# Six instead of four of a batch's sixteen chunks weighted on ScalarE in a graph-attention stage

## What is computed

```python
x_proj = (x @ W).reshape(n, H, D)            # H = 8 heads, D = 32
alpha_src = jnp.einsum('nhd,hd->nh', x_proj, a_src)
alpha_dst = jnp.einsum('nhd,hd->nh', x_proj, a_dst)
e = alpha_src[row] + alpha_dst[col]
m = jax.ops.segment_max(e, col, num_segments=n)
e_exp = jnp.exp(e - m[col])
s = jax.ops.segment_sum(e_exp, col, num_segments=n)
att = e_exp / (s[col] + 1e-16)
out = jax.ops.segment_sum(att[:, :, None] * x_proj[row], col, num_segments=n)
```

## Time and profile before

| what | value |
|---|---|
| median of 3 runs | 3672.1 us (3669.44 to 3673.27) |
| profiled execution, its own time | 3671.94 us |
| its span | 3670.2 us |
| span, share busy: PE, DVE, ACT, POOL | 76%, 50%, 26%, 47% |
| granted PE clock, mean | 0.875 of full speed |

### The profile page before, as it was taken

One profiled execution on the slowest core, in us unless ns is written; L12 is line 12 of the kernel. 1 busy time (PEld: TensorE's weight loads), 2 busy tenths in 40 slices (PEclk: granted clock), 3 DMA queues, 4 the chain that ended last, 5 costly groups with the idle time before them and its releaser, 6 DMA issues. The chain is left out here.

```text
span 3670.2 us, 56109 instructions
## 1 busy us (share of the span) xinstructions
PE 2801.8 (76%) x13194; PEld 2306.5 (63%) x13195; DVE 1850.6 (50%) x4258; ACT 965.1 (26%) x3415; POOL 1719.0 (47%) x1811
## 2 busy tenths in 40 slices
PE   1477888887874999999995647766776776738999
PEld 0356666666663888888884535555555555538998
DVE  5324454444556111111113758778887778773444
ACT  0001110000010222222221334333443333325554
POOL 0677777777770222232221177766666667200000
PEclk9888888888887999999997868888888888857999
DMA  5333333333330222222222543333333333100000
GB/s 170 94 105 110 110 116 110 110 109 110 109 108 15 81 81 86 83 86 83 85 84 84 171 110 106 104 103 101 100 102 103 102 102 104 43 17 9 20 21 20
DMA packets 152206, 327.38 MB, mean 89 GB/s; under 512 B 38743, under 2 KB 89905, under 8 KB 147938
## 3 DMA queue, kind: packets, MB, share of 16 engines
q0 software_dynamic: 85824, 236.38, 22.8%
q1 hardware_dynamic: 59762, 83.04, 6.8%
q10 hardware_dynamic: 6480, 6.42, 0.5%
HBM read 286.42 MB, written 41.40 MB: 89 GB/s over the span
## 5 line engine op out<-in xcount | busy, mean ns | idle before, releaser
L633 POOL DMA_INDIRECT G<-g_rows,srcT x784 | 743.1, 948 | 426.3 <-issue 237.2
L633 POOL DMA_INDIRECT G<-h_rows,srcT x784 | 752.3, 960 | 251.8 <-issue 237.0
L1728 PE MATMUL pS<-G,O 128*128 x2336 | 639.2, 437 | 56.9 <-DVE O L1876 55.8
L817 PE MATMUL pS<-G,O 128*128 x2336 | 569.7, 408 | 142.2 <-SPq L804 108.6
L817 PEld LDWEIGHTS pS<-G,O 128*128 128x128 f32 x2336 | 476.4, 206 | 231.9 <-issue 153.3
L1728 PEld LDWEIGHTS pS<-G,O 128*128 128x128 f32 x2336 | 492.6, 214 | 199.4 <-issue 83.3
L1361 PE MATMUL pH<-XT,w1s 128*128 128x256 f32 x1728 | 384.0, 381 | 0.9 <-DVE XT L1401 0.9
L1371 PE MATMUL pY<-w2s,HE 128*128 128x256 f32 x1728 | 381.9, 379 | 0.0
L1361 PEld LDWEIGHTS pH<-XT,w1s 128*128 128x128 f32 x1728 | 329.8, 191 | 46.5 <-issue 1.3
L1386 ACT ACTIVATE HE<-pH,b1s 128x256 f32<-128x256 f32 x432 | 204.9, 474 | 583.2 <-PE pH L1361 583.2
L1293 POOL DMA_INDIRECT y_rows<-YE,yidx x108 | 109.3, 1012 | 527.3 <-DVE YE L1413 510.8
(11 more groups left out here) (301 smaller groups left out, 3535.2 us busy)
## 6 DMA issues: line engine op xcount, KB each, us to landing
w1s<-in_W_dram SPq DMA_DIRECT2D x16, 1024.0 KB, 5.2
w2s<-in_W_dram SPq DMA_DIRECT2D x16, 1024.0 KB, 8.0
G<-h_rows,srcT POOLq DMA_INDIRECT x784, 2.7
Y<-y_rows SPq DMA_DIRECT2D x49, 256.0 KB, 4.4
G<-g_rows,srcT POOLq DMA_INDIRECT x784, 2.8
g_rows<-OUT SPq DMA_DIRECT2D x49, 132.0 KB, 2.5
h_rows<-ACC SPq DMA_DIRECT2D x7, 896.0 KB, 5.4
X<-in_x_dram SPq DMA_DIRECT2D x1, 6144.0 KB
```

The lines of the kernel that those rows point to most:

```text
L633: pool.indirect_dma_start(out=G[:, c % (ring * Q), 0:width], out_offset=None, in_=rows, in_offset=bass.IndirectOffsetOnAxis(ap=srcT[:, c:c ...
L817: mm = nc.tensor.matmul(pS[k][:, 0:W], O[:, k, q, :], G[:, bass.ds((s % R0) * Q + q, 1), :].rearrange("p a d -> p (a d)"), start=(q == 0), ...
L1728: mm = nc.tensor.matmul(pS[:, bass.ds((w % BANKS) * BANK, NR)], O[:, k, q, :], G[:, bass.ds((s % R) * Q + q, 1), 0:NR].rearrange("p a d -> ...
```

## The change

`SHARE`, the number of chunks of a batch that ACT weights, goes from 4 to 6. DVE's one instruction then covers 10 chunks instead of 12 (2560 elements per partition instead of 3072), and ACT issues 48 instructions per batch instead of 32. Nothing else is edited.

```diff
             RB = R // z.BS
-            SHARE = 4
+            SHARE = 6
             PAIR_STEPS = 12
```

## The result

The changed kernel takes 3640.82 us (median of 6, 3638.37 to 3646.55) against 3671.32 us for the kernel before on the same chip: a ratio of 0.9916, 95% interval 0.9906 to 0.9926, or 30.5 us less. The forecast was 3639 us, the range 3628 to 3657. The profiled execution has a span of 3639.0 us, 31.2 less than before.

A forecast was written before the change was run, and what follows sets the result against it. The prediction took the stage from batch 3 on to be one chain on DVE. DVE's shorter chain (25 us) plus PE's clock (8 us) made 33 us off 3672.1, giving 3639 us, range 3628 to 3657.

The forecast's parts named there:

- DVE's saving: L1950 on DVE loses 512 of 3072 elements at 1.038 ns each: 0.53 us per batch.
- slow pairs: PE's second pairs taking 9.32 us instead of 7.64, in 14 batches of two pairs; DVE then waits about 1.2 us.
- It counts from batch 2 on: L1950's saving is lost to gather waits in batches 0 and 1, counts in batches 2 to 48: 25 us.
- ACT's work costs nothing: ACT's block grows 3.44 us per batch to 10.32, inside its 5.25 us idle before `fac`; costed at nothing.
- The overhead: Between ACT's block and `fac`: waiting for its products, signalling PE and entering the loop, between 0 and 1.58 us.
- The cover of 1.30 us: DVE first reads `fac` in L1858, 1.30 us after it ended, so a `fac` 0.30 us late is covered.
- The Trainium skill's rule: Puts multiplications on VectorE, not ScalarE, so speaks against the change; if the moved work lay on the chain, 143 us more.
- The last batch: Without DVE's scans `fac` comes 2.4 to 4.0 us late, 3.6 of it covered: 0 to 0.4 us, taken as 0.
- PE's clock: Shorter idle before PE's second pairs leaves fewer at the low clock: 8 us gained, bounds 17 gained to 12 lost.
- The long batches: Batches of two pairs lasting 26.59 to 26.71 us instead of 25.39, in 14 cases.
- Gathers: Rival: POOL's gathers bind in the one-pair batches and take the gain back, 3668 us; chance 0.06.
- Slower by a late `fac`: Rival: ACT's longer block holds `fac` back, DVE held up 1.8 us per batch, 3733 us; chance 0.04.

The follow-up runs named there:

- e1: Changed kernel (six chunks on ACT) with two dummy products on DVE behind L1950, some 0.53 us per batch: 3670.94 us, ratio 0.9991 to the kernel before.
- e6: Changed kernel (six chunks on ACT) with four dummy 128x128 products on PE at the start of each pair: 3639.38 us, ratio 0.9913 to the kernel before.
- e5: Kernel before (four chunks on ACT) with four dummy 128x128 products on PE at the start of each pair: 3658.46 us, ratio 0.9967.
- e3: Changed kernel with SHARE set to seven chunks on ACT instead of six: 3628.07 us, ratio 0.9873 to the kernel before.
- e4: Changed kernel with SHARE set to eight chunks on ACT instead of six: 3699.49 us, ratio 1.0068 to the kernel before.
- e2: Changed kernel (six chunks on ACT) with four chunks in the last batch alone: 3640.14 us, ratio 0.9910 to the kernel before.
- e10: Kernel before (four chunks) with two dummy products on DVE behind L1950, some 0.53 us longer per batch: 3688.46 us, ratio 1.0044.
- e11: Kernel before (four chunks) with one dummy product on DVE behind L1950, some 0.27 us longer per batch: 3682.98 us, ratio 1.0031.

## Why the prediction was right, and where not

- *DVE's saving.* Worked out 0.53 us per batch, measured 3356 - 2823 = 533 ns. e1 shows that it is the cause; e6 against e5 shows it without slow pairs (22.2 us).
- *It counts from batch 2 on.* EX(2) came 0.75 us earlier only, and L1950 still waited 24.6 us in four places, nearly all in batches 0 to 2. Right but for batch 2 itself, where L1950's wait grew from 2.16 to 2.75 us and took its saving back.
- *ACT's work costs nothing.* Block 10.27 us (10.32 worked out), rest 1.33 (1.28). The overhead, bounded by 0 and 1.58 us, is 0.33. The cover of 1.30 us is shown by e3 (used, not exceeded) and e4 (exceeded, 1.70 us each). Right. The Trainium skill's rule, page "ScalarE: Activation LUTs", section "Rules for kernel authors", which puts multiplications on VectorE, did not decide. The rows bear out its order and no more: a chunk takes 1.72 us on ACT and 0.27 on DVE, but e3 carries seven chunks on ACT at a gain.
- *The last batch* was the step that failed: 0 to 0.4 us was costed, 2.69 came. The working had `fac` right (DVE waited 1.44 us for it), but it took the 2.26 us that DVE next waits for PE as room. It overlooked that PE's products of the last batch come directly behind that batch's weighting, so that `s_prep_act`, elsewhere a batch early, is the last to arrive. PE started 3.06 us later, and DVE's wait for it grew to 3.38. PE's 9.30 us wait names it, e2 removes it.
- *PE's clock*: +8 was taken, 8.5 to 9.1 remain by subtraction and 10.9 by e5 and e6, but the reason given was wrong. Not every idle before a second pair shrank: the longest fell from 2.82 to 2.37 us, that of batch 26 grew from 1.35 to 1.59, since PE's first pair keeps its start but not its length. The counts of 14, 2, 5 and 0 to 2 for four to seven chunks, and 11 and 2 with DVE made longer, follow no order in DVE's time. The long batches were also read too narrowly, from two of them: the 14 last 26.57 to 27.04 us, not 26.59 to 26.71. What is shown: the slow pairs exist, cost up to 14 us in the kernel before (e5), come with a granted clock of 0.82 in the second pair (1.00 in the pairs of 7.64 us), and change in number with the batches' length. What isn't: why the low clock lies where it does, and how to tell their number ahead. The value fell well by luck inside bounds that were rightly kept at -12 to +17.
- *Gathers* did not take the gain back: the score copies waited for them five times before and five times after (60.2 and 57.8 us in all), and POOL's wait still stands at 50.8 us. *Slower by a late `fac`*: DVE waited for `fac` in L1858, which the prediction had named as a sign of being wrong, but only in the last batch.

## What to carry to other kernels

When an engine's program is the chain, price what it sheds by its own slope and look at the receiving engine's first reader: idle behind the block, plus how long the result lies before it is read, is the room there is; with the 0.33 us that the run with six showed, it gave seven as the most here before seven and eight were run. Look at the last iteration by itself, because what is a whole iteration early in the loop can be last there; a different split for that iteration alone took 5.5 us off the tail with seven chunks. And a wait for an engine is room only if that engine isn't itself held back by the change. Where another engine's clock rises and falls within the loop, give its term both signs: taking 0.53 us off DVE's chain cut the slow pairs from 14 to 5, but taking 0.27 off e10's raised them from 2 to 11 (e11).

## What was not expected of the hardware

Four useless products per pair (the trace shows eight) on an engine that had idle time made the kernel 0.33% faster: no second pair ran at the lower granted clock any more (1.00 instead of 0.82 in batch 32). And a loop that was made 0.53 us longer per batch lost 12 of its 14 slow pairs, at no higher a mean clock. Batch 0's EX, ahead of which all the kernels run the same code, lay between 2119.8 and 2126.5 us in the profiles, so differences of a few microseconds between single runs of this kernel need the profile's own stretches to be read.
